# One router kernel, one change: first tiles' rows gathered singly, last routing steps moved forward

## The chip, the core and the metric

The kernel runs on one core of a Trainium2 chip. A core has five engines with an instruction stream each: TensorE (PE, matrix products), VectorE (DVE), ScalarE (ACT), GpSimd (POOL) and SyncE (SP, here used to start transfers). They meet only through semaphores. The metric is the device time of one execution in microseconds (us), lower is better; a kernel's time is the median of its runs.

## What is computed

A block with adaptive layer norm on 2048 tokens of width 512, all in float32: a small state layer (`tanh(h B^T) C^T + D h`), then a mixture of experts with 8 experts of width 352, of which each token takes two, and a shared part of two halves, each as wide as an expert.

```
mod = (silu(c) @ wmod).reshape(.., 6, 1, -1)          # sa, ca, ga, sb, cb, gb
h = layernorm(x) * (1 + ca) + sa
x = x + ga * (tanh(h @ B.T) @ C.T + D * h)
h = layernorm(x) * (1 + cb) + sb
scores = sigmoid(h @ gate_w.T);  idx = top_k(scores + router_bias, 2)
w = scores[idx] / sum(scores[idx])
y_e = (silu(h @ W1[e]) * (h @ W3[e])) @ W2[e]
x = x + gb * (sum over the two of w * y_e + shared(h))
```

## The kernel before

The 2048 tokens are 16 tiles of 128, worked in 8 pairs. Each float32 product is made of three matmuls of high and low parts (hi*hi, hi*lo, lo*hi), so each operand is split into a high part by ACT and a low part by DVE before TensorE can use it.

**Stage A** (to about 211 us) is a software pipeline over the pairs, `body(it, lo, hi)` on every engine, with iterations 0 to 10. In iteration `it` the pair `it-2` gets its state product and its second norm (`h2`), the pair `it-3` its transposes of h2 (`transposes`, L905), the split of the result (ACT `xah`, DVE `xal`), and the first shared half: `up`, `silu`, product `gbuf`, transposes of `g` (`turn_g`, L943), split `gth`/`gtl`, `down`. The pair `it-4` is routed: on DVE `route` in 12 small steps (0 to 6 before, 7 to 11 behind the matmuls of `ranks` on TensorE), which gives the rows to which POOL scatters the tokens of the pair in the DRAM tensor `xs` (`scatter`, four indirect DMAs a pair, L601). The rows of h2 to scatter are read back by SyncE into `hrow` (L406). In the last iteration POOL also starts the weights of the first expert: `raw` (2.2 MB) and the high parts `whi` in three pieces (`hi_part`).

**Stage B** is four steps, tiles 0 to 3 with the second shared half. Step 0 still has the last A tile's down product, and the last pair's ranks and `route`. In step 1 DVE builds `table_rows`, in step 2 `table_rest` (16 small instructions; its last one raises `s_tab`, on which POOL's `low`, the low parts of the first expert's weights, waits). In step 3 TensorE transposes the first tile of the scattered rows, loaded by SyncE when all scatters have landed (L448, L389).

**Stage S** runs all the expert tiles, some 6.7 us a step, and stores each result to the DRAM tensor `ys`.

**Stage C** (from about 485 us) is twelve steps (c,j), pairs c = 2 to 7, j = 0, 1, with the second shared half of tiles 4 to 15. POOL gathers the two expert results of each tile, `tbuf` and `xtf`, 128 rows each (`gather`, L684). The rows of the tiles 0 to 3 of stage B (`rowb`, in `raw`) are gathered too (`gather_first`, L691), two gathers a tile. One step (c,j) on DVE, in program order: low part of the next tile (`tlo`, L1349), `gbuf` (L1596), half of a `finish_first` (tile t: half 0 waits for both gathers of the tile, half 1 ends it; the halves run in steps (3,1), (4,0), (4,1), (5,0), ... (7,0)), `gtl` (L1610), `finish` of the tile before (four instructions, L1560 to L1567), and `offsets`, which writes the row numbers of the next tile (`idx`, L1528) that POOL's next `gather` waits for. TensorE in a step: transposes of the next tile, `up`, `down` of the tile before, `turn_g`. ACT enters a loop (`Fori`) at step (4,0).

Every engine works its stream in the written order. All of POOL's DMAs share one software queue, SyncE's another.

Of the kernel before, what the change touches and what calls it, by code (L numbers as in the profile page):

```python
# [35 lines left out]
NT = T // P  # L36
# [15 lines left out]
CB = 2  # L52
# [25 lines left out]
def build(nc, x, ccol, wmod, bt, ct, dvec, gwt, rb, w_all, consts, out):  # L78
# [4 lines left out]
    with ExitStack() as ctx:  # L83
# [404 lines left out]
        def _(pool):  # L488
# [60 lines left out]
            def body(it, lo, hi):  # L549
# [54 lines left out]

                if routes(lo, hi):
                    scatter(it - 4, 0)
                if lo == NP + 2:
                    hi_part(0, lambda: pool.wait_ge(q["A", "up"], NT))
                    hi_part(1, lambda: None)
                    scatter(it - 3, 1)  # L610
                    hi_part(2, lambda: pool.wait_ge(q["A", "dn"], NT))
# [76 lines left out]
            def gather_first(t):  # L688
                pool.wait_ge(s_bidx, 1)
                for k in range(2):  # L690
                    pool.indirect_dma_start(rowb[t][:, k, :], None, ys[:, :],  # L691
                                            bass.IndirectOffsetOnAxis(ap=idxb[:, 2 * t + k:2 * t + k + 1], axis=0)
                                            ).then_inc(s_brow[t], 16)
# [3 lines left out]
            for t in range(NB):  # L697
                gather_first(t)
                if t % 2:
                    for j in range(2):  # L700
                        gather(CB + 1 + t // 2, j)
            with pool.Fori(CB + 1 + NB // 2, NP) as c:
                for j in range(2):
                    gather(c, j)


        @block.scalar
        def _(act):
            def high(i, j, src):
                act.wait_ge(q["S", "xt"], i * 2 + (j + 1))  # L710
                act.activation(xbh[:, j, :], src[:, :], ACT.Copy).then_inc(q["S", "xhi"], 1)  # L711

            def hidden(p, j, lo):
                n = p * 2 + (j + 1)
                act.wait_ge(q["A", "up"], n)
                if lo > 3 or j:
                    act.wait_ge(q["A", "g"], p * 2 + j)
                act.activation(s1[:, :], bank[2][:, E:E + F], ACT.Silu).then_inc(q["A", "silu"], 1)
                act.activation(lg[:, bass.ds(p * 2 + j, 1), :].rearrange("p a e -> p (a e)"), bank[2][:, 0:E],
                               ACT.Copy).then_inc(s_lg, 1)  # L720
                if lo == NP + 2 and j == 1:
                    high(0, 0, bank[6])
                act.wait_ge(q["A", "gt"], n)
                if lo > 3 or j:
                    act.wait_ge(q["A", "dn"], p * 2 + j)
                act.activation(gth[:, :], bank[4 + j][:, 0:FP], ACT.Copy).then_inc(q["A", "ghi"], 1)
# [36 lines left out]
            def body(it, lo, hi):  # L763
                if live(1, lo, hi):
                    turned(it - 1, lo)
                if live(3, lo, hi):
                    p = it - 3
                    act.wait_ge(s_h2T, p + 1)
                    if lo > 3:
                        act.wait_ge(q["A", "up"], p * 2)  # L770
                    for j in range(2):
                        act.activation(xah[:, j, :], h2_bank(lo, j)[:, :], ACT.Copy).then_inc(q["A", "xhi"], 1)
                    if lo > NP:
                        scores(p - 1)
                    if lo == 3:
                        first_weights(2)
                    hidden(p, 0, lo)
# [10 lines left out]
                if live(3, lo, hi):  # L788
                    hidden(it - 3, 1, lo)
                    if lo not in (NP, NP + 1):  # L790
                        scores(it - 3)
# [77 lines left out]
        def _(pe):  # L869
# [128 lines left out]
            def body(it, lo, hi):  # L998
                if live(1, lo, hi):
                    turn_t(it - 1, lo)  # L1000
                if live(3, lo, hi):
# [37 lines left out]
                if live(3, lo, hi):  # L1039
                    pe.wait_ge(s_lg, (it - 3) * 2 + 1)  # L1040
                    up("A", it - 3, 1, 0)
                if lo == NP + 2:
                    turn(0, 0, bank[6])
# [9 lines left out]
                if routes(lo, hi):  # L1053
# [36 lines left out]
            def step(i, j, c, sec):  # L1090
# [23 lines left out]
                up("S", i, j, off, [NW + 1, NW + 2] if sec == "B" else need_up)  # L1114
                if early:
                    next_turn()
                if first:
                    ranks(NP - 1)
# [31 lines left out]
        def _(dve):  # L1150
# [200 lines left out]

            def body(it, lo, hi):
# [6 lines left out]
                if live(3, lo, hi):  # L1359
                    p = it - 3  # L1360
                    for j in range(2):
                        dve.wait_ge(q["A", "xhi"], p * 2 + (j + 1))
                        dve.tensor_tensor(xal[:, j, :], h2_bank(lo, j)[:, :], xah[:, j, :].bitcast(F32),  # L1363
                                          ALU.subtract).then_inc(q["A", "xlo"], 1)
# [80 lines left out]
                if live(3, lo, hi):  # L1445
                    product_a(it - 3, 1, lo)
                if lo == NP + 2:
                    lows(0, 0, bank[6])
                if live(3, lo, hi):
# [3 lines left out]
                between(*range(KM + 1, KR))  # L1453
# [117 lines left out]
            def step(i, j, c, sec):  # L1571
# [13 lines left out]
                if sec == "B" and i * 2 + j == 2:  # L1585
                    table_rest()
# [7 lines left out]
                else:  # L1594
                    dve.wait_ge(q["S", "gt"], i * 2 + j)
                dve.tensor_tensor(gbuf[:, 0:F], s1[:, :], bank[3][:, 0:F], ALU.mult).then_inc(q["S", "g"], 1)  # L1596
                m = (c - CB) * 2 + j - 3 if sec == "C" else -1
# [4 lines left out]
                if first:  # L1602
                    route(NP - 1, NP + 3, *range(KM + 1, KR))
# [94 lines left out]
```

## Time and profile before

| what | value |
|---|---|
| median of 3 runs | 583.18 us (582.14 to 585.02) |
| profiled execution: its own time | 589.56 us |
| profiled execution: span | 587.9 us |
| busy in the span | PE 547.9 us (93%), DVE 303.7, POOL 260.7, ACT 178.2 |
| mean granted TensorE clock | 0.981 |
| DMA moved | 107.18 MB, mean 182 GB/s |
| longest ACT wait | s L849, 10.1 us, at 499 us |
| longest POOL wait | tbuf L684, 45.3 us, for the last store of stage S |

The times are all of one profiled execution unless a median is named; a row of a timeline is start, duration, engine, line, operation, output and input, and in square brackets how long the engine was idle before it and what released it. The profiled execution took 6.4 us longer than the median. PE is busy in tenths of 9 in all but a few of the 40 slices of the page: the first four or so, and the 35th and 36th, 500 to 529 us.

### The profile page before, as it was taken

What the parts mean: (1) busy time and instruction counts of PE and PEld (TensorE: products, weight loads), DVE (VectorE), ACT (ScalarE), POOL (GpSimd) and SP (SyncE); (2) the same over time, 40 slices, a digit from 0 to 9 for tenths busy, and PEclk for the clock granted to TensorE, in tenths of its full rate; (3) what the DMA queues carried; (4) which work ended last, traced back from release to release, by engine and by line L of the source; (5) the groups of instructions that cost most, each with busy time, mean ns of one, the idle gap of its engine ahead of it and who ended that gap; (6) DMA issues with size and microseconds to landing.
All of it is one profiled execution on the core that took longest, in us unless ns stands there. A gap on an engine that the chain in (4) does not pass through costs nothing.

```text
span 587.9 us, 11157 instructions
## 1 busy us (share of the span) xinstructions
PE 547.9 (93%) x3176; PEld 494.7 (84%) x3177; DVE 303.7 (52%) x633; ACT 178.2 (30%) x343; POOL 260.7 (44%) x219
## 2 busy tenths in 40 slices
PE   5986799999999898999999999999999999679995
PEld 2655788998899897899999999999999999579994
DVE  3589876686687567433222232222222222457886
ACT  1242345345524432123222332222322223112220
POOL 1598876667665527442053420162633002451331
PEclk9998999999999999999999999999999999798999
DMA  8988244332232578556266762548484223672644
GB/s 307 394 297 317 72 186 173 127 115 81 89 144 105 200 260 272 206 195 225 89 191 236 254 227 91 168 144 321 143 321 141 73 71 106 180 215 78 190 144 142
DMA packets 38040, 107.18 MB, mean 182 GB/s; under 512 B 4224, under 2 KB 4224, under 8 KB 36992
## 3 DMA queue, kind: packets, MB, share of 16 engines
q1 hardware_dynamic: 28288, 54.44, 26.8%
q0 software_dynamic: 9728, 52.43, 25.9%
q8 instruction: 14, 0.23, 0.2%
q14 instruction: 10, 0.08, 0.1%
HBM read 76.19 MB, written 30.67 MB: 182 GB/s over the span
## 4 chain that ended last, share of the span: by engine, by line
PE 77%; POOL 8%; issue 5%; DVE 4%; DMA 2%; another core or an unknown queue 1%; ACT 1%; SPq 0%; DVEq 0%; ACTq 0%; POOLq 0%
PE bank L922 14%; PE bank L923 13%; PE bank L924 13%; PE bank L938 7%; PE bank L936 7%; PE bank L937 7%; PE bank L905 5%; PE bank L943 4%; PE bank L874 2%; PE bank L876 2%; PE bank L875 2%; PE bank L883 1%; POOL xs_rows L601 1%; DMA x_all<-wmod 1%
## 5 line engine op out<-in xcount | busy, mean ns | idle before, releaser
L922 PE MATMUL bank<-whi,thi 128*128 (+1 forms) x416 | 140.9, 339 | 0.0
L923 PE MATMUL bank<-wlo,thi 128*128 (+1 forms) x416 | 136.1, 327 | 0.0
L924 PE MATMUL bank<-whi,tlo 128*128 (+1 forms) x416 | 135.6, 326 | 0.0
L531 POOL TENSOR_TENSOR wlo<-raw,whi 128x1408 f32 (+3 forms) x24 | 79.6, 3331 | 85.9 <-DMA whi<-w_all 74.4
L1596 DVE TENSOR_TENSOR gbuf<-s,bank 128x352 f32<-128x352 f32 x52 | 27.1, 521 | 112.2 <-ACT s L849 107.5
L936 PE MATMUL bank<-whi,gth 128*128 (+1 forms) x204 | 80.7, 396 | 3.3 <-DVE wlo L1320 2.0
L938 PE MATMUL bank<-whi,gtl 128*128 (+1 forms) x204 | 80.5, 395 | 0.0
L922 PEld LDWEIGHTS bank<-whi,thi 128*128 128x128 f32 x416 | 80.0, 192 | 0.0
L923 PEld LDWEIGHTS bank<-wlo,thi 128*128 128x128 f32 x416 | 79.9, 192 | 0.0
L937 PE MATMUL bank<-wlo,gth 128*128 (+1 forms) x204 | 79.8, 391 | 0.0
L924 PEld LDWEIGHTS bank<-whi,tlo 128*128 128x128 f32 x416 | 79.6, 191 | 0.0
L849 ACT ACTIVATE s<-bank 128x352 f32<-128x352 f32 x52 | 24.2, 466 | 165.4 <-PE bank L924 148.0
L1610 DVE TENSOR_TENSOR gtl<-bank,gth 128x384 fp32r<-128x384 f32 x52 | 29.0, 558 | 84.5 <-ACT gth L857 83.0
L857 ACT ACTIVATE gth<-bank 128x384 fp32r<-128x384 f32 x52 | 25.6, 492 | 100.8 <-PE bank L943 91.2
L684 POOL DMA_INDIRECT tbuf<-ys_rows,idx x12 | 11.5, 958 | 90.3 <-DMA ys_rows<-tmpa 45.3
L936 PEld LDWEIGHTS bank<-whi,gth 128*128 128x128 f32 x204 | 38.3, 188 | 9.5 <-DVE wlo L1320 2.3
L938 PEld LDWEIGHTS bank<-whi,gtl 128*128 128x128 f32 x204 | 38.3, 188 | 8.9
L905 PE MATMUL bank<-cst,h 128*128 128x128 f32 x272 | 41.8, 283 | 4.2 <-DMA h<-xs_rows 2.8
L922 PE MATMUL bank<-whi,xah 128*128 128x360 f32 (+1 forms) x128 | 42.4, 331 | 2.8 <-DVE xal L1363 2.7
L1349 DVE TENSOR_TENSOR tlo<-bank,thi 128x512 fp32r<-128x512 f32 x52 | 35.8, 689 | 17.6 <-ACT thi L711 17.2
L943 PE MATMUL bank<-cst,gbuf 128*128 128x128 f32 x204 | 34.1, 276 | 10.6 <-DVE gbuf L1596 9.4
L943 PEld LDWEIGHTS bank<-cst,gbuf 128*128 128x128 f32 x204 | 26.3, 140 | 20.8 <-DVE gbuf L1596 10.7
(199 smaller groups left out, 982.5 us busy)
## 6 DMA issues: line engine op xcount, KB each, us to landing
raw<-w_all POOLq DMA_DIRECT2D x8, 2176.0 KB, 9.3
whi<-w_all POOLq DMA_DIRECT2D x16, 704.0 KB
h<-xs_rows SPq DMA_DIRECT2D x36, 256.0 KB
ys_rows<-tmpa SPq DMA_DIRECT2D x36, 256.0 KB, 2.0
x_all<-wmod SPq DMA_DIRECT2D x6, 1024.0 KB, 8.5
whi<-w_all POOLq DMA_DIRECT2D x8, 768.0 KB, 4.8
hs_rows<-h SPq DMA_DIRECT2D x8, 512.0 KB, 3.0
h<-hs_rows SPq DMA_DIRECT2D x16, 256.0 KB
```

The costliest lines, as they stand in the source:

```text
L531: pool.tensor_tensor(wlo[:, bass.ds(off + (SH + a), b - a)], raw[:, a:b], whi[:, bass.ds(off + (SH + a), b - a)].bitcast(F32), ALU.subtrac ...
L905: mm = pe.transpose(dst[:, k * P:(k + 1) * P], src[:, k * P:(k + 1) * P], ident)
L922: pe.matmul(dst, xh[:, j, a], wh, start=(m == 0), stop=False)
L923: pe.matmul(dst, xh[:, j, a], wl, start=False, stop=False)
L924: mm = pe.matmul(dst, xl[:, j, a], wh, start=False, stop=(m == KD - 1))
L936: pe.matmul(dst, gth[:, a], wh, start=(m == 0), stop=False)
L937: pe.matmul(dst, gth[:, a], wl, start=False, stop=False)
L938: mm = pe.matmul(dst, gtl[:, a], wh, start=False, stop=(m == KF - 1))
L943: mm = pe.transpose(dst[:, m * P:(m + 1) * P], gbuf[:, m * P:(m + 1) * P], ident)
L1349: dve.tensor_tensor(xbl[:, j, :], src[:, :], xbh[:, j, :].bitcast(F32), ALU.subtract).then_inc(q["S", "xlo"], 1)
L1596: dve.tensor_tensor(gbuf[:, 0:F], s1[:, :], bank[3][:, 0:F], ALU.mult).then_inc(q["S", "g"], 1)
L1610: dve.tensor_tensor(gtl[:, :], bank[4][:, 0:FP], gth[:, :].bitcast(F32), ALU.subtract).then_inc(q["S", "glo"], 1)
```

## The change

- POOL's code for stage C: `gather_first(t)`, which issued both gathers of one of the tiles 0 to 3, and ran for two tiles in a row (four DMAs) ahead of a pair's gathers, becomes `gather_first(t, k)`, one DMA, placed behind each of the eight gathers of (3,0) to (6,1). The loop over the last pairs is written out.
- Iteration 9 of stage A: the transposes of the last pair's h2, and their splits on ACT and DVE, come in iteration 9 behind the second `up` rather than at the start of iteration 10. ACT's `scores` of the last pair comes ahead of `gth`.
- Iteration 10: the matmuls of `ranks(6)` and DVE's steps 7 to 11 of that pair are ahead of the down product. POOL issues the first two high parts of the first expert's weights ahead of the scatter of pair 6 rather than behind it.
- Stage B: `ranks(7)` and `route(7, 7..11)` are ahead of the turn and of `gbuf` in step 0. `table_rest` comes in step 1, right behind `gbuf`, rather than in step 2.

```diff
 (POOL, iteration 10)
+                if lo == NP + 2:
+                    hi_part(0, lambda: pool.wait_ge(q["A", "up"], NT))
+                    hi_part(1, lambda: None)
                 if routes(lo, hi):
                     scatter(it - 4, 0)
                 if lo == NP + 2:
-                    hi_part(0, lambda: pool.wait_ge(q["A", "up"], NT))
-                    hi_part(1, lambda: None)
                     scatter(it - 3, 1)
...
 (POOL, stage C)
             for j in range(2):
                 gather(CB, j)
-            for t in range(NB):
-                gather_first(t)
-                if t % 2:
-                    for j in range(2):
-                        gather(CB + 1 + t // 2, j)
-            with pool.Fori(CB + 1 + NB // 2, NP) as c:
+            for c in range(CB + 1, NP):
                 for j in range(2):
                     gather(c, j)
+                    n = (c - CB - 1) * 2 + j
+                    if n < 2 * NB:
+                        gather_first(n // 2, n % 2)
...
 (ACT, hidden)
+                if lo == NP + 1 and j == 1:
+                    high_a(NP - 1, lo)
                 if lo == NP + 2 and j == 1:
                     high(0, 0, bank[6])
+                    scores(NP - 1)
                 act.wait_ge(q["A", "gt"], n)
...
 (PE, body)
+                if lo == NP + 1:
+                    pe.wait_ge(s_h2, NT)
+                    pe.wait_ge(q["A", "xlo"], NT - 2)
+                    pe.wait_ge(q["A", "glo"], NT - 3)
+                    for j in range(2):
+                        mm = transposes(h2_bank(lo, j), h2[:, j, :])
+                    mm.then_inc(s_h2T, 1)
                 if lo == NP + 2:
+                    ranks(it - 4)
                     turn(0, 0, bank[6])
...
 (PE, step)
+                if first:
+                    ranks(NP - 1)
                 if early:
                     next_turn()
                 if first:
-                    ranks(NP - 1)
                     last_tile(NP - 1, NP + 3)
...
 (DVE, body)
+                if lo == NP + 1:
+                    lows_a(NP - 1, lo)
                 if lo == NP + 2:
                     lows(0, 0, bank[6])
+                    between(*range(KM + 1, KR))
...
 (DVE, step)
-                if sec == "B" and i * 2 + j == 2:
-                    table_rest()
...
+                if first:
+                    route(NP - 1, NP + 3, *range(KM + 1, KR))
                 dve.tensor_tensor(gbuf[:, 0:F], s1[:, :], bank[3][:, 0:F], ALU.mult).then_inc(q["S", "g"], 1)
+                if sec == "B" and i * 2 + j == 1:
+                    table_rest()
...
                 if first:
-                    route(NP - 1, NP + 3, *range(KM + 1, KR))
                     finish_a(NP - 1, 1, NP + 3)
```

POOL's instructions of stage C, as the program before has them, from the gathers of (2,0) on (`tbuf` and `xtf` are a tile's two gathers, `raw` a gather of `gather_first`):

```order
L684 DMA tbuf<-ys_rows,idx 128x512
L684 DMA xtf<-ys_rows,idx 128x512
L684 DMA tbuf<-ys_rows,idx 128x512
L684 DMA xtf<-ys_rows,idx 128x512
L691 DMA raw<-ys_rows,idxb 128x512 x4
L684 DMA tbuf<-ys_rows,idx 128x512
L684 DMA xtf<-ys_rows,idx 128x512
```

and as the changed program has them:

```order
L685 DMA tbuf<-ys_rows,idx 128x512
L685 DMA xtf<-ys_rows,idx 128x512
L685 DMA tbuf<-ys_rows,idx 128x512
L685 DMA xtf<-ys_rows,idx 128x512
L685 DMA tbuf<-ys_rows,idx 128x512
L685 DMA xtf<-ys_rows,idx 128x512
L691 DMA raw<-ys_rows,idxb 128x512
L685 DMA tbuf<-ys_rows,idx 128x512
L685 DMA xtf<-ys_rows,idx 128x512
L691 DMA raw<-ys_rows,idxb 128x512
```

The four gathers that stood ahead of those of (3,0) are now one by one, each behind a tile's own two. The second gather of tile 0 stands behind the gathers of (3,1), where it stood ahead of (3,0).

DVE in steps 1 and 2 of stage B before (the first `tlo` is the low part of tile 2, `tqi` to the last `ti` is `table_rest`):

```order
L1596 TENSOR_TENSOR gbuf<-s,bank 128x352
L1349 TENSOR_TENSOR tlo<-bank,thi 128x512
L1610 TENSOR_TENSOR gtl<-bank,gth 128x384
L1533 TENSOR_TENSOR bank<-bank,mods 128x512
L1535 TENSOR_TENSOR x_all<-bank,x_all 128x512
L1349 TENSOR_TENSOR tlo<-bank,thi 128x512
L1296 TENSOR_SCALAR tqi<-tq 1x41
L1297 TENSOR_SCALAR ti<-tq 1x40
...
L1314 TENSOR_SCALAR ti<-tr 1x10
L1596 TENSOR_TENSOR gbuf<-s,bank 128x352
```

and in the changed program:

```order
L1616 TENSOR_TENSOR gbuf<-s,bank 128x352
L1310 TENSOR_SCALAR tqi<-tq 1x41
...
L1328 TENSOR_SCALAR ti<-tr 1x10
L1363 TENSOR_TENSOR tlo<-bank,thi 128x512
L1631 TENSOR_TENSOR gtl<-bank,gth 128x384
L1553 TENSOR_TENSOR bank<-bank,mods 128x512
L1555 TENSOR_TENSOR x_all<-bank,x_all 128x512
L1363 TENSOR_TENSOR tlo<-bank,thi 128x512
L1616 TENSOR_TENSOR gbuf<-s,bank 128x352
```

All of `table_rest` now stands between `gbuf` of step 1 and the low part of tile 2.

## Rows read from the trace of the kernel before

**Rows 1.** Timeline of PE, 195 to 245 us: start us, us, instruction, [idle before <-releaser]

```profile
198.01 0.40 PE L922 MATMUL bank<-whi,xah 128*128 128x360 f32 x1 [1.80 <-DVE xal L1363]
...
234.61 1.09 PE L905 MATMUL bank<-cst,h 128*128 128x128 f32 x4 [2.77 <-DMA h<-xs_rows]
...
240.28 0.39 PE L936 MATMUL bank<-whi,gth 128*128 128x512 f32 x1
...
242.69 0.60 PE L905 MATMUL bank<-cst,h 128*128 128x128 f32 x4
```

**Rows 2.** One-microsecond windows: busy us (instructions) by engine, PEclk, DMA share, GB/s

```profile
198.00:199.00 1.00, 0.99 (x6) 1.00 (x7) 0.57 (x2) 0.97 (x3) 0.92 (x1) 1.00 1.04 401
...
236.00:237.00 1.00, 1.00 (x5) 1.00 (x5) 0.50 (x1) 0.40 (x1) 1.00 (x2) 0.50 0.03 8
```

**Rows 3.** Timeline of DVE, 224 to 231 us

```profile
224.30 0.68 DVE L1349 TENSOR_TENSOR tlo<-bank,thi 128x512 fp32r<-128x512 f32 x1
...
228.11 0.17 DVE L1296 TENSOR_SCALAR tqi<-tq 1x41 int32<-1x41 f32 x1
...
230.22 0.50 DVE L1596 TENSOR_TENSOR gbuf<-s,bank 128x352 f32<-128x352 f32 x1
```

**Rows 4.** Timeline of POOL, 202 to 217 us

```profile
202.92 0.59 POOL L496 DMA_DIRECT2D raw<-w_all  x1
...
215.55 1.00 POOL L601 DMA_INDIRECT xs_rows<-mods,idx  x1 [12.03 <-DVE oh L1226]
```

**Rows 5.** Timeline of SyncE's DMA queue, 205 to 206 us

```profile
205.56 0.38 SPq L406 DMA_DIRECT2D mods<-hs_rows  x1
```

**Rows 6.** Chain that ended last, 225 to 235 us: start us, us, what

```profile
225.86 4.95 DMA xs_rows<-tmpa,idx
...
231.81 2.67 DMA h<-xs_rows
```

**Rows 7.** Timeline of ACT, 498 to 528 us

```profile
509.19 0.46 ACT L849 ACTIVATE s<-bank 128x352 f32<-128x352 f32 x1 [10.09 <-remote]
...
527.70 0.46 ACT L849 ACTIVATE s<-bank 128x352 f32<-128x352 f32 x1 [7.29 <-remote]
```

**Rows 8.** Timeline of PE from 497 us: the transposes of g

```profile
497.54 0.49 PE L943 MATMUL bank<-cst,gbuf 128*128 128x128 f32 x3
...
510.26 0.90 PE L943 MATMUL bank<-cst,gbuf 128*128 128x128 f32 x3 [5.87 <-DVE gbuf L1596]
...
528.77 0.90 PE L943 MATMUL bank<-cst,gbuf 128*128 128x128 f32 x3 [3.02 <-DVE gbuf L1596]
...
558.35 0.49 PE L943 MATMUL bank<-cst,gbuf 128*128 128x128 f32 x3
...
571.73 0.49 PE L943 MATMUL bank<-cst,gbuf 128*128 128x128 f32 x3
```

**Rows 9.** Timeline of DVE, 501 to 552 us

```profile
501.80 0.75 DVE L1560 SCALAR_TENSOR_TENSOR tmpa<-tbuf,wts,bank 128x512 f32<-128x512 f32 x1 [2.65 <-issue]
...
545.96 0.56 DVE L1610 TENSOR_TENSOR gtl<-bank,gth 128x384 fp32r<-128x384 f32 x1 [0.58 <-ACT gth L857]
546.43 0.74 DVE L1560 SCALAR_TENSOR_TENSOR tmpa<-tbuf,wts,bank 128x512 f32<-128x512 f32 x1
...
549.33 0.21 DVE L1528 CAST idx<-pos 128x1 uint32<-128x1 f32 x2
...
550.27 0.52 DVE L1596 TENSOR_TENSOR gbuf<-s,bank 128x352 f32<-128x352 f32 x1
...
551.22 0.75 DVE L1543 SCALAR_TENSOR_TENSOR raw<-raw,wts 128x512 f32<-128x512 f32 x1
```

**Rows 10.** Timeline of POOL, 550 to 553 us

```profile
550.30 1.01 POOL L684 DMA_INDIRECT tbuf<-ys_rows,idx  x1 [4.10 <-DVE idx L1528]
551.61 1.18 POOL L684 DMA_INDIRECT xtf<-ys_rows,idx  x1 [0.30 <-issue]
```

**Rows 11.** Half-microsecond window, columns as in group 2

```profile
555.00:555.50 0.50, 0.50 (x5) 0.50 (x5) 0.47 (x2) 0.00 (x0) 0.00 (x0) 1.00 0.00 0
```

## What I expect of the change

> **What bounds the kernel now.** I read the page's slices first, then the waits, then the timelines of the places where PE is not busy. PE is busy for 547.9 of 587.9 us, so a change can gain only where PE waits, and can lose wherever it makes PE wait. Three places matter.
>
> At 198.01 PE has waited 1.80 us for the low part of the last pair's h2 [rows 1]; the granted clock stayed at 1.00, 2.4 GHz [rows 2]. At 234.61 it has waited 2.77 us for the first tile of scattered rows, which SyncE loads when the last scatter has landed [rows 1, 6]. The clock fell there: 0.50 in 236 to 237 us, 1.2 GHz [rows 2]. From this turn to the next down product it took 240.28 - 234.61 = 5.67 us; at full clock it is a step of 6.69 less 242.69 - 240.28 = 2.41, so 4.28. The slow clock cost 1.4 us on top of the wait.
>
> In stage C, PE's transposes of g came 12.72 us apart at 510.26, and the two steps after that took 18.51 us, where two undisturbed ones take 571.73 - 558.35 = 13.38 [rows 8]. From 497.54 to 571.73 there are nine steps: 74.19 us, where 9 x 6.69 = 60.2 are due, so 14.0 us are lost. In both disturbed steps it is ACT's `silu` that came late, at 509.19 and 527.70, and what it waited for is no engine ("remote") [rows 7]. I take it for ACT's own code being fetched by DMA while POOL keeps the DMA engines busy: the first wait ends when the traffic of POOL's ten gathers in a row does, the second begins at ACT's entry into its loop and ends with the traffic of the next eight. The Trainium skill (Runtime: NRT & Kernel Launch, Instruction fetch mechanics) says that each engine streams its code over a DMA queue of its own and that a taken branch out of the loaded pages forces a fetch before work goes on; by that rule, too, fewer gathers ahead of the fetch shorten the wait, and the loop entry keeps one.
>
> **The change, front part (stages A and B).**
>
> 1. The last h2 transposes, one product earlier. TensorE does the same eight transposes, ACT's two splits fall in the time in which it waits for `gt`, DVE's two in its wait for the down product. So the wait of 1.80 us goes [rows 1]: -1.80 at 198 us. The clock had not fallen, so nothing is to be had from it.
>
> 2. `table_rest` in step 1. It takes 230.22 - 228.11 = 2.11 us [rows 3], and now stands ahead of the low part of tile 2, which `up` of step 2 waits for. Before, that low part started at 224.30, right behind `gbuf`, and ended at 224.98. Now it is 224.30 - 1.80 + 2.11 + 0.68 = 225.3. That gives back the 1.80: of step 1 some 0 to 0.2 us stay, I take 0.1. PE is then free for the first scattered tile at 234.61 - 2.77 - 0.1 = 231.7.
>
> 3. The scatters. POOL's queue has the 2.2 MB `raw` from 202.92, SyncE reads the rows of pair 6 from 205.56, and the scatter of pair 6 starts at 215.55 [rows 4, 5]. DVE's row numbers are put down as its releaser, but those of pair 6 had been there for two microseconds; I take the rows' landing for it, 10.0 us behind their issue, because both transfers share the engines. Routing earlier (ranks, steps 7 to 11) is then worth nothing for pair 6. And two `whi` pieces, 1.4 MB, are now queued in those ten microseconds instead of between the scatters. The rows' load also moves by some 0.8 us, since pair 5's routing stands behind the splits moved in 1. So pair 6 can start at 216.4 at the earliest and, if all of `whi` must pass first (3.6 us at the 401 GB/s of a busy window, [rows 2]), at 220; I take 217. The eight scatters take 225.86 + 0.96 - 215.55 = 11.3 us to issue [rows 4, 6], of which some 1.5 are the two `whi` issues between them: 226.8. Before, the last landed 4.0 us behind its issue (4.95 less 0.96, [rows 6]), behind 1.4 MB of `whi`. Those are gone, and pair 5's landed in 205.56 - 202.92 = 2.6 [rows 4, 5]: 229.4. SyncE's start and load cost 3.7 more, as before (231.81 + 2.67 against 230.8): 233.1, so the turn comes 1.5 us earlier than 234.61. The remaining gap, 1.4 us, is under the 1.80 that left the clock alone, so the 1.4 of the slow clock comes back as well. Front part: **-2.9**. Best case, everything in time at 231.7: -4.3. Worst, 220 + 9.8 + 4.0 + 3.7 = 237.5: +2.9.
>
> Stage S runs at PE's pace, 6.69 us a step, and passes that on unchanged.
>
> **The change, stage C.** The ten gathers in a row become four, and six from there on come in threes. In the frame of the trace before:
>
> 4. Step (3,0). `finish` of (2,0) still starts at 501.80, `idx` 2.90 later (546.43 to 549.33, [rows 9]), `gbuf` 0.94 after that: 505.6. ACT, with four gathers ahead instead of ten, should have its code by then. PE's transposes come at 506.2 rather than 510.26, and the clock should hold. `gtl` comes 1.9 us behind `gbuf` (turn_g, ACT's `gth`, hand-overs), `finish` 0.47 behind it [rows 9], so `idx` of (3,1) at 510.9.
>
> 5. A new wait, and it is the main thing. Half 0 of `finish_first` in step (3,1) waits for both gathers of tile 0. The second is now issued behind the two gathers of (3,1), and those wait for the `idx` that DVE has written at the end of the step before. So DVE waits, in the middle of its step, for three gathers that it has itself only just let go; behind this wait are queued `gtl` (PE's down), `finish`, `idx` and the next `gbuf`. The same holds for tiles 1, 2, 3 in (4,1), (5,1), (6,1). In us from `idx`: POOL starts 0.97 later (550.30 - 549.33); the two gathers need 551.61 + 1.18 - 550.30 = 2.49 [rows 10], the third 1.25: 4.71. Landing: the second gather of this pair was issued by 552.79 and no byte moves after 555.0 [rows 11], so 2.2: at 6.9. Bounds 1.7 (the same half-microsecond window) and 4.0 (the last scatter, [rows 6]). At present half 0 is done at 551.22 + 0.75 and starts some 0.43 behind `gbuf`'s start, 1.4 us behind `idx` [rows 9]; so DVE stands still for 5.5.
>
> 6. The period of two steps. From 6.9: half 0 ends 1.27 later (551.97 less 550.70, [rows 9]), `finish` starts 0.47 later, `idx` 2.90: 11.55. `gbuf` 0.94: 12.5. `gtl` 1.9 (half 1 fits in): 14.4. 0.47 and 2.90: 17.75. This is a closed loop of DVE and POOL, **17.75 us for two steps against 13.38** of PE. PE waits some 2.2 us for `gtl` and 2.2 for `gbuf` in each. Three such periods from 510.9 give `idx` of (6,1) at 564.15; `gbuf` of (7,0) at 576.65, transposes 0.55 later at 577.2 against 571.73: **+5.5** in which the removed 14.0 are already counted.
>
> 7. The clock in these gaps. 1.80 us left it, 2.77 did not; 2.2 twice, 2.1 us apart, lies between. I take it to fall. Most of that hides behind the loop, which doesn't contain `up`; the last `up`, behind (7,0), isn't hidden: +1.4, bounds 0 and 2.1 (18.51 - 13.38 - 3.02, what the clock cost after 510.26).
>
> The Trainium skill (DMA: Bandwidth & Descriptors, Anatomy of one DMA) gives some 2.0 us plus bytes over 436 GB/s for one DMA of GpSimd, 2.6 us for 262 KB; counted from the issue's start that is 1.65 behind its end, and the sum would be 2.2 us lower.
>
> **Sum.** -2.9 + 5.5 + 1.4 = +4.0 us: span 591.9, and that execution 593.6. The median of the runs is 6.4 below the profiled execution; if nothing of this is in the places above, the median goes from 583.18 to **587.2**. If part of ACT's two waits is longer only under the profiler, there is less to gain and as much to lose, so the error from this is upward.
>
> **Rivals.**
> - *Faster: the third gather lands almost at once.* With each gather issued in 0.95 and the third landed 1.0 behind its issue, each of the four waits is 1.5 us shorter: 4 x 1.5 = 6.0, so -2.0, and the clock holds: -3.4, **579.8**. For it: spaced gathers have the DMA engines nearly to themselves. Against it: the last pair's traffic ran for 2.2 us. It decides from a landing under 1.2 us.
> - *Even: same loop, cheap ends.* Landing 1.7, clock holds, front best: 5.5 - 2.0 - 4.3 = -0.8, **582.4**.
> - *ACT's late code has nothing to do with the gathers*, so the change doesn't do what it says: `gbuf` of (3,0) stays at 509.7, 4.1 later, and the loop follows: **591.3**. Against it: both waits end with the gathers.
> - *Landing 4.0*, with SyncE's loads and stores in the way: 4 x 1.8 = 7.2 more, **594.4**.
>
> **How the numbers follow.** Forecast 0.40, faster 0.17, even 0.25, ACT unchanged 0.10, slow landing 0.08. About 0.5% is what a measurement of this kernel tells from no change, 2.9 us; the forecast is at 0.7%, and I put 0.06 of it within. So slower 0.52, same 0.31, faster 0.17. The range goes from 579.5, just past the faster case, to 593.0, short of slow landing.
>
> **What would show it.** In the trace of the changed kernel: no idle PE near 196; a wait of 1.7 us at `up` of step 2; the first scattered tile's turn at about 233; ACT's `silu` of (3,0) within 505; DVE waits of some 5.5 us at L1561, four of them, each two steps apart; PE's transposes of g 17.7 us apart by twos. The prediction is wrong if these four waits are under 4 us, if a fetch of ACT's still ends later than the third gather, or if the scattered tile comes later than 234.6.

## The result, and the profile of the changed kernel

| | kernel before | changed kernel |
|---|---|---|
| median of 4 runs | 584.10 us (582.14 to 587.17) | 594.12 us (593.92 to 594.86) |
| profiled execution, own time | 589.56 us | 593.92 us |
| its span | 587.9 us | 592.3 us |

The ratio is **1.0169, with a 95% interval of [1.0121, 1.0217]**: slower, as forecast, but 594.12 us lies above the forecast of 587.2 and 1.1 us above the range. Span against span the change cost 592.3 - 587.9 = 4.4 us, where the sum said 4.0. That the two agree so closely is partly luck, since misses of the sum's terms cancel, but the loop that sets the end came as described. What failed is the step from the profiled execution of before to the medians: the median rose by 10.0 us, not by 4.0.

The page of the changed kernel: span, busy times, PE's busy tenths and the granted clock in 40 slices.

```profile
span 592.3 us, 11140 instructions
PE 548.8 (93%) x3176; PEld 492.5 (83%) x3177; DVE 302.9 (51%) x633; ACT 178.4 (30%) x343; POOL 259.3 (44%) x219
...
PE   5986799999999997999999999999999999887885
...
PEclk9998999999999999999999999999999999999799
```

PE's holes now lie in the last six slices; before they were in the 35th and 36th. In DVE's waits (engine, line, releaser: us in total, times, longest) there is an entry that the kernel before doesn't have:

```profile
DVE raw L1561 <- DMA raw<-ys_rows,idxb: 21.6, 4, 6.0
```

The same four in DVE's timeline (columns as in [rows 9]):

```profile
517.23 0.48 DVE L1561 TENSOR_SCALAR raw<-raw,wts 128x512 f32<-128x512 f32 x1 [5.97 <-DMA raw<-ys_rows,idxb]
...
534.67 0.49 DVE L1561 TENSOR_SCALAR raw<-raw,wts 128x512 f32<-128x512 f32 x1 [5.66 <-DMA raw<-ys_rows,idxb]
...
552.20 0.49 DVE L1561 TENSOR_SCALAR raw<-raw,wts 128x512 f32<-128x512 f32 x1 [5.74 <-DMA raw<-ys_rows,idxb]
...
570.12 0.49 DVE L1561 TENSOR_SCALAR raw<-raw,wts 128x512 f32<-128x512 f32 x1 [4.25 <-DMA raw<-ys_rows,idxb]
```

They end 17.44, 17.53 and 17.92 us apart: the period of two steps, forecast as 17.75. POOL's timeline shows the other half of the loop:

```profile
528.59 0.94 POOL L685 DMA_INDIRECT tbuf<-ys_rows,idx  x1 [2.17 <-DVE idx L1548]
529.84 0.95 POOL L685 DMA_INDIRECT xtf<-ys_rows,idx  x1 [0.30 <-issue]
531.10 0.95 POOL L691 DMA_INDIRECT raw<-ys_rows,idxb  x1 [0.30 <-issue]
```

DVE's `idx` lets three gathers go; the third, for which DVE then stands, is issued from 531.10 on. The chain that ended last says when such gathers landed (start us, us from issue to landing):

```profile
513.21 4.00 DMA raw<-ys_rows,idxb
531.10 3.55 DMA raw<-ys_rows,idxb
```

The second is 531.10 + 3.55 = 534.65, and DVE goes on at 534.67. PE pays twice in each period, once for `gtl` and once for `gbuf`. Its transposes of g, and the down product that waits for `gtl` (these are the rows that answer to [rows 8]):

```profile
497.57 0.49 PE L948 MATMUL bank<-cst,gbuf 128*128 128x128 f32 x3
...
505.25 0.55 PE L948 MATMUL bank<-cst,gbuf 128*128 128x128 f32 x3 [0.83 <-DVE gbuf L1616]
...
519.11 0.49 PE L941 MATMUL bank<-whi,gth 128*128 x1 [2.17 <-DVE gtl L1631]
...
523.07 0.55 PE L948 MATMUL bank<-cst,gbuf 128*128 128x128 f32 x3 [1.62 <-DVE gbuf L1616]
...
540.51 0.55 PE L948 MATMUL bank<-cst,gbuf 128*128 128x128 f32 x3 [1.61 <-DVE gbuf L1616]
...
558.04 0.90 PE L948 MATMUL bank<-cst,gbuf 128*128 128x128 f32 x3 [0.88 <-DVE gbuf L1616]
...
575.97 0.55 PE L948 MATMUL bank<-cst,gbuf 128*128 128x128 f32 x3 [1.61 <-DVE gbuf L1616]
```

From 497.57 to 575.97 there are nine steps, 78.40 us; in [rows 8] the same nine took 74.19. ACT's `silu` never waits for "remote" here; the row that answers to the first of [rows 7] stands at 502.38, not 509.19, and waits for PE:

```profile
502.38 0.47 ACT L854 ACTIVATE s<-bank 128x352 f32<-128x352 f32 x1 [3.25 <-PE bank L929]
```

In the front part, first POOL's scatter of pair 6 ([rows 4]), then PE's `up` of step 2 and the turn of the first scattered tile ([rows 1]):

```profile
217.75 1.13 POOL L601 DMA_INDIRECT xs_rows<-mods,idx  x1 [9.78 <-DMA mods<-hs_rows]
```

```profile
225.47 0.40 PE L927 MATMUL bank<-whi,thi 128*128 128x352 f32 x1 [1.76 <-issue]
...
234.42 0.94 PE L910 MATMUL bank<-cst,h 128*128 128x128 f32 x4 [2.47 <-DMA h<-xs_rows]
...
242.71 0.49 PE L910 MATMUL bank<-cst,h 128*128 128x128 f32 x3
```

The wait at 198 us is gone, the 1.76 us at 225.47 are new (due to `table_rest`), and the turn stands 0.19 us earlier than before. The turn after it is at 242.71, where it was at 242.69: the front part brought nothing.

### The profile page after: what moved, and what is told of

It is laid out like the page before. It is cut to its first block, busy times and chain, and to the rows that moved or that the text cites. A ratio compares the mean times of both kernels' runs of the same rounds, so it can differ in the third digit from the quotient of the medians.

```text
span 592.3 us, 11140 instructions
## 1 busy us (share of the span) xinstructions
PE 548.8 (93%) x3176; PEld 492.5 (83%) x3177; DVE 302.9 (51%) x633; ACT 178.4 (30%) x343; POOL 259.3 (44%) x219
## 4 chain that ended last, share of the span: by engine, by line
PE 68%; POOL 10%; DMA 8%; DVE 7%; issue 6%; ACT 1%; SPq 0%; DVEq 0%; POOLq 0%; ACTq 0%
PE bank L927 12%; PE bank L928 12%; PE bank L929 12%; PE bank L943 6%; PE bank L941 6%; PE bank L942 6%; PE bank L910 4%; PE bank L948 3%; DMA raw<-ys_rows,idxb 3%; DMA mods<-hs_rows 2%; PE bank L881 2%; PE bank L879 2%; PE bank L880 2%; POOL xs_rows L601 2%; PE bank L888 1%
## 5 line engine op out<-in xcount | busy, mean ns | idle before, releaser
L942 PEld LDWEIGHTS bank<-wlo,gth 128*128 128x128 f32 x204 | 38.5, 189 | 6.1
```

Of the source, the lines that this page charges most:

```text
L942: pe.matmul(dst, gth[:, a], wl, start=False, stop=False)
```

## Experiments

Theory 1 is that the loop of DVE and POOL is the whole cost and the front part is worth nothing. In its first form, held for `b_again`, `g_only`, `f_only` and `g_ahead`, it still counted most of the 14.0 us lost in [rows 8] as part of the kernel before, so it put the loop at 1.5% to 1.9% and expected a gain from the single gathers placed ahead; both were missed. From `b_again2` on it says that the 14.0 us belong to single executions, not to the kernel, and that the loop costs some 17.5 us against an execution without them. The rival keeps the prediction's reading: ACT's late code is part of the kernel before, brought about by its bursts of gathers. "Late code" stands here for ACT's two waits for "remote" in [rows 7]; that code is what ACT waited for is the prediction's reading. The experiments ran on three chips (that of the first comparison is not on record), each kernel beside runs of the kernel before, to which its ratio refers.

### The kernel before, unchanged, profiled again

> The kernel before, unchanged, profiled a second time. Its first profiled execution took 589.56 us where its runs have a median of 584.1; the changed kernel's profiled execution took 593.92, its median 594.12. Theory 1: the difference lies in the two waits of ACT for its own code in stage C, whose length differs from execution to execution. Then an execution near 583 shows PE's transposes of g from the end of stage S to (7,0) in about 68 us rather than 74.2, and the front up to the first scattered tile unchanged at 234.6. Theory 2: the difference lies in the front part (start, scatters): then the 74.2 stay and the first scattered tile's turn is some 6 us earlier.

576.31 us, span 574.7, against 589.56 and 587.9. Its ACT and PE (columns as in [rows 7] and [rows 8]):

```profile
501.04 0.47 ACT L849 ACTIVATE s<-bank 128x352 f32<-128x352 f32 x1 [3.25 <-PE bank L924]
```

```profile
496.23 0.49 PE L943 MATMUL bank<-cst,gbuf 128*128 128x128 f32 x3
504.81 0.55 PE L943 MATMUL bank<-cst,gbuf 128*128 128x128 f32 x3 [1.73 <-DVE gbuf L1596]
...
558.47 0.49 PE L943 MATMUL bank<-cst,gbuf 128*128 128x128 f32 x3
```

The ten gathers stand in a row, and no `silu` is late. Nine steps take 62.24 us, so 2.0 are lost and not 14.0. Of the 13.2 us between the two spans, 74.19 - 62.24 = 11.9 lie in these nine steps and 1.3 ahead of them (497.54 against 496.23). So the place is the one theory 1 named, but the execution is shorter by more than either theory had expected. The rival falls here: a burst of gathers alone doesn't make ACT's code late.

> The kernel before once more. Its first profiled execution had ACT's silu at 13.5 and 10.8 us instead of 6.7 us behind the one before it at two steps of stage C, and 14.0 us lost there; its second (b_again) had neither, 2.0 us lost, and was 13 us shorter. If the late code belongs to single executions, this one shows anything between: 2 to 14 us lost over the nine steps from (2,1) to (7,0), and its own time is 574 plus what is lost over 2.0. If something else makes the kernel's times differ, the lost time and the execution's own time do not move together.

On another chip 575.92 us, span 574.3; its nine steps take 558.07 - 496.51 = 61.56 us, so 1.4 are lost, just under the 2 to 14 expected.

> The kernel before, unchanged, a third look. Two looks in the experiments had no late ACT code and spans of 574.3 to 574.7 us. Theory 1 (the 14.0 us that the first profiled execution lost to ACT's late code belong to single executions, not to the kernel): this look too is either free of them, span 573 to 576 us, or, if the late code shows, its span is 10 to 14 us longer with ACT's first wait near 499 us. Rival (the late code is a steady part of the kernel that the two looks missed by chance): it shows, at 499 us and at the entry into the loop.

On a third chip 575.47 us, span 573.8: 557.64 - 495.13 = 62.51 us for the nine steps, 2.3 lost. All three executions agree within 0.9 us of span, and none has a `silu` that is released by "remote". So the late code wasn't seen again. That it is not a steady part of the kernel is shown, on three chips; why the first profiled execution had it is not.

### The gathers alone

The kernel before, with only this, and with `gather_first(t, k)` issuing one gather where `gather_first(t)` issued two:

```diff
-            for t in range(NB):
-                gather_first(t)
-                if t % 2:
-                    for j in range(2):
-                        gather(CB + 1 + t // 2, j)
-            with pool.Fori(CB + 1 + NB // 2, NP) as c:
+            for c in range(CB + 1, NP):
                 for j in range(2):
                     gather(c, j)
+                    n = (c - CB - 1) * 2 + j
+                    if n < 2 * NB:
+                        gather_first(n // 2, n % 2)
```

> The kernel before with the changed gathers of stage C alone; the front as before. Theory 1 (the loop of DVE and POOL costs the time, the front is worth nothing): ratio 1.015 to 1.019, as the whole change, and four DVE waits of 4 to 6 us in stage C, two steps 17.5 us apart. Rival (the front part costs some of the 10 us): 1.005 to 1.012.

596.06 us (594.05 to 598.72) beside 577.70: ratio 1.0335 [1.0275, 1.0396], far above the 1.015 to 1.019 expected, the whole of the loss and more than the first comparison showed for the whole change. Its span, 592.4, is 17.7 above that of `b_again` on the same chip. In DVE's waits:

```profile
DVE raw L1538 <- DMA raw<-ys_rows,idxb: 23.6, 4, 6.3
```

### Half of them late

Tiles 0 and 1 as in the kernel above, tiles 2 and 3 ahead of the tile's own two gathers. Against that kernel:

```diff
-                    gather(c, j)
                     n = (c - CB - 1) * 2 + j
+                    if NB <= n < 2 * NB:
+                        gather_first(n // 2, n % 2)
+                    gather(c, j)
-                    if n < 2 * NB:
+                    if n < NB:
                         gather_first(n // 2, n % 2)
```

> The changed gathers on the kernel before, but for the tiles 2 and 3 each single gather stands ahead of its tile's two, so that only the tiles 0 and 1 are waited for. By the loop of DVE and POOL two of the four periods of two steps stay at 17.5 us and two fall back to 13.4: 8.5 us over the kernel before, ratio 1.013 to 1.018 where the whole of it gave 1.0335. If the waits were not what costs (the written-out loop, more DMAs a step), it stays near 1.03.

585.41 us, ratio 1.0148 [1.0121, 1.0176]. In DVE's waits two of the three are long, of 6.35 and 5.83 us; the third is 0.21:

```profile
DVE raw L1540 <- DMA raw<-ys_rows,idxb: 12.4, 3, 6.4
```

Two waits cost 583.5 - 574.3 = 9.2 us of span, four cost 17.7: 4.4 to 4.6 us of the end for each wait of some 5.9. By the medians it is 585.41 - 576.83 = 8.6 for two and 596.06 - 577.70 = 18.4 for four, 4.3 to 4.6 each. Half the waits cost half the time. A cause that goes with the number of gathers or with the written-out `Fori` loop alone would give both kernels the same time, since these two differ in nothing but the order of four gathers.

### All of them ahead

Against the kernel of "The gathers alone":

```diff
                 for j in range(2):
-                    gather(c, j)
                     n = (c - CB - 1) * 2 + j
                     if n < 2 * NB:
                         gather_first(n // 2, n % 2)
+                    gather(c, j)
```

> The kernel before with the eight single gathers, each placed ahead of the two gathers of its tile instead of behind them, so that both rows of tile t are gathered one step before DVE asks for them. If the four waits are what costs, they vanish, and with them the long bursts: two steps are 13.4 us apart throughout, about 2 us of the 14.0 stay at (3,0): in the profile 576 to 578 us of span, against the median of before a ratio of 0.985 to 0.992 (theory 1). If single gathers cost by themselves (three DMAs in each step against the DVE's finish), the ratio stays at 1.00 or above.

575.66 us, ratio 0.9996 [0.9963, 1.0029], span 572.8. The waits are gone as expected; the expected gain (0.985 to 0.992) is not there. DVE has no wait for `raw` at all. POOL and DVE in the same stretch:

```profile
505.18 0.94 POOL L690 DMA_INDIRECT raw<-ys_rows,idxb  x1 [0.30 <-issue]
508.45 0.96 POOL L684 DMA_INDIRECT tbuf<-ys_rows,idx  x1 [2.33 <-DVE idx L1525]
```

```profile
508.82 0.48 DVE L1538 TENSOR_SCALAR raw<-raw,wts 128x512 f32<-128x512 f32 x1
```

The gather that `finish_first` needs at 508.82 is issued at 505.18, ahead of the wait for DVE's next `idx`, which ends at 508.45. The same eight single gathers, between the same others, cost nothing when they stand two places earlier in the queue. They also gain nothing over the bursts: the expected gain was most of the 14.0 us, and the undisturbed kernel loses only 1.4 to 2.3.

### The front part alone

The changed kernel with POOL's code for stage C as it was before.

> The changed kernel with the old gathers of stage C: the front part alone. Its share by the changed kernel's trace: the turn of the first scattered tile at 234.42 against 234.61, so nothing: ratio 0.998 to 1.002. My prediction's term was -2.9 us: 0.995. Rival (whi ahead of the scatters delays them in undisturbed runs): 1.003 or more.

576.71 us, ratio 0.9992 [0.9965, 1.0019]. The turn, in PE's timeline:

```profile
225.24 0.40 PE L930 MATMUL bank<-whi,thi 128*128 128x352 f32 x1 [1.76 <-issue]
234.26 0.63 PE L913 MATMUL bank<-cst,h 128*128 128x128 f32 x4 [2.53 <-DMA h<-xs_rows]
```

The kernel before has its turn at 233.82, 234.91 and 233.22 in its three other executions: the same place. The front part moves steps around and meets the same transfers.

### The front part without the two `whi` pieces moved

Against the kernel of the section before (so with the old gathers too):

```diff
-                if lo == NP + 2:
-                    hi_part(0, lambda: pool.wait_ge(q["A", "up"], NT))
-                    hi_part(1, lambda: None)
                 if routes(lo, hi):
                     scatter(it - 4, 0)
                 if lo == NP + 2:
+                    hi_part(0, lambda: pool.wait_ge(q["A", "up"], NT))
+                    hi_part(1, lambda: None)
```

> The front part of the change with the two whi pieces back between the scatters; old gathers. If whi ahead of the scatter of pair 6 is what delayed it (217.75 against 215.55), it starts at 215.5 to 216 again. The last scatter then again lands behind 1.4 MB of whi, so the first scattered tile's turn comes within 0.5 us of the kernel before's: ratio 0.998 to 1.002. A ratio under 0.996 would mean that moving whi alone spoiled the front part.

579.91 us, ratio 1.0049 [1.0024, 1.0074], where 0.998 to 1.002 was expected. The scatter of pair 6 starts at 216.11, 1.5 us earlier than with the `whi` pieces ahead of it (217.58 in `f_only`), but the last one lands later, as the chain shows (start us, us to landing):

```profile
220.89 5.21 DMA whi<-w_all
226.23 5.38 DMA xs_rows<-tmpa,idx
232.62 2.61 DMA h<-xs_rows
```

5.38 from the start of the issue against 3.61 in the changed kernel. The turn comes at 235.36 with a gap of 3.05, and the granted clock falls to 0.50. So of the front part, moving `whi` ahead seems worth something: the two ratios are 0.57% or some 3 us apart, and the rest of the front part takes about as much away. The two were measured on different chips, and how much of the 3 us is this fall of the clock is not shown.

### Everything forward, the weights behind the scatters

The changed kernel with the gathers ahead, `table_rest` back in step 2, and POOL's `raw` and first two `whi` behind both scatters:

```diff
-                    fetch_raw(0)
...
-                if lo == NP + 2:
-                    hi_part(0, lambda: pool.wait_ge(q["A", "up"], NT))
-                    hi_part(1, lambda: None)
                 if routes(lo, hi):
                     scatter(it - 4, 0)
                 if lo == NP + 2:
                     scatter(it - 3, 1)
+                    fetch_raw(0)
+                    hi_part(0, lambda: pool.wait_ge(q["A", "up"], NT))
+                    hi_part(1, lambda: None)
```

> Single gathers ahead of each tile's two, the h2 transposes and the routing moved forward as in the changed kernel, but table_rest back in step 2, and raw and whi of the first expert issued only behind both scatters. If the rows of pair 6 land late because raw is in flight (10 us for 0.5 MB), they land in under 5 us now, the scatters start at 210 to 211, the last lands by 224, and the first scattered tile's turn comes without a wait at 229.7 to 231: 3 to 4 us less than before, ratio 0.992 to 0.996. If the load of the first scattered tile is slowed by raw instead, the wait of 2 us at the turn stays and the ratio is 0.997 to 1.001.

575.95 us, ratio 0.9990 [0.9972, 1.0008]: no difference that can be told. The chain:

```profile
207.02 3.08 DMA h<-hs_rows
210.10 0.96 POOL xs_rows L600
...
219.47 2.73 DMA xs_rows<-tmpa,idx
223.20 8.86 DMA h<-xs_rows
```

The scatter starts at 210.10, where it was 217.75 in the changed kernel, 217.58 in `f_only` and 216.11 with only the `whi` pieces moved back. The rows to scatter are not what it waits for here. They come with SyncE's load issued at 205.56 before and at 205.59 here; the last number is us from issue to landing, first before, then here:

```profile
mods<-hs_rows SPq DMA_DIRECT2D x1, 512.0 KB, 9.2
```

```profile
mods<-hs_rows SPq DMA_DIRECT2D x1, 512.0 KB, 3.5
```

So without `raw` they are there at 209.1, and pair 6's row numbers at 209.30. The 210.10 is the landing of another load, `h<-hs_rows`, for which POOL's code still waits at the place where `raw` stood. In the kernel before the rows landed at 205.56 + 9.2 = 214.8, and the scatter started 0.8 us later; in the changed kernel it is 216.96 and 217.75. This shows what the prediction had only taken: the rows' landing, slowed by the 2.2 MB, was what held pair 6. But the load of the scattered rows now runs beside `raw` itself and takes 8.86 us instead of 2.68, so the turn is at 232.20, with a gap of 2.46. In both places that were tried for the weights, a small load that is waited for stood beside them.

### The changed kernel again, and with its gathers ahead

> The changed kernel, unchanged. Theory 1 (its loop of DVE and POOL sets stage C in every execution, and only the kernel before has executions with and without late code): 594 to 597 us, as in its first runs (594.12) and as the kernel with the gathers alone (596.06), four DVE waits of 5.5 to 6 us for raw, and a ratio of 1.028 to 1.036 against the kernel before on the same chip, rather than the 1.017 of the first runs. Rival (the first chip was slower by some 1.5% for both kernels alike): the changed kernel comes at 585 to 588 us here, with a ratio of 1.015 to 1.020.

595.05 us (593.29 to 597.21) beside 578.11 (575.05 to 580.93, 13 runs): ratio 1.0312 [1.0266, 1.0357]. The changed kernel takes nearly the same in both comparisons, 594.12 and 595.05. It is the kernel before that differs: 584.10 in the first comparison, 578.11 here. A first chip that makes both kernels slower alike is ruled out with that.

> The changed kernel with the single gather ahead of each tile's two rather than behind, so that it is let go a step before DVE needs it; all the rest of the change stays. Theory 1 (the place of the gather is the whole loss, the front part is worth nothing): no DVE wait for raw over 1 us, 573 to 578 us, ratio 0.996 to 1.002. Rival (the front part and the gathers cost something together, for instance by code or transfers that fall into each other): ratio over 1.004.

579.09 us, ratio 1.0030 [1.0008, 1.0051]. The loss goes from 3.1% to 0.3% by the order of eight instructions; there is no DVE wait for `raw`. The rest is between what the theories said (up to 1.002, and over 1.004), and is not settled by the one trace. There the clock fell twice, at the turn (235.08, gap 2.67) and in (3,0):

```profile
506.97 0.55 PE L948 MATMUL bank<-cst,gbuf 128*128 128x128 f32 x3 [1.86 <-DVE gbuf L1616]
...
515.31 0.49 PE L948 MATMUL bank<-cst,gbuf 128*128 128x128 f32 x3
```

That is 8.34 us for a step of 6.69. No version beat the kernel before by more than its measurement can tell.

## Why the prediction was right and wrong

The way back from the trace, span against span, with the profiled execution of before: front 0.0, nine steps of stage C 78.40 - 74.19 = +4.2, and the rest +0.2.

The terms of the sum were -2.9, +5.5 and +1.4 and measured 0.0, +4.2 and, within the last 0.2, some +0.1. Their misses of +2.9, -1.3 and -1.3 nearly cancel, and that is luck.

- **Steps 1 and 2 held.** The wait at 198 us went, `up` of step 2 waits 1.76 us instead (1.7 forecast), the low part of tile 2 starts at 224.69, 0.4 us later than before, and so ends within 0.1 of the 225.3 forecast. Together nothing.
- **Step 3 held in its mechanism, not in its size.** Pair 6 starts at 217.75 (217 forecast) and waits for the rows. The last issue ends at 226.99 + 0.96 = 227.95 (226.8), the landing takes 2.65 more (2.6), and SyncE and the load 3.8 (3.7): 234.42 instead of 233.1. That left a gap of 2.47 instead of 1.4, and the clock fell as before: 0.0 for a forecast -2.9. What was missed is small, 0.75 us of start and 0.4 of issue, but it carried the gap over the 1.80 on which the -1.4 of the clock hung. Even that condition was too simple: in `after_again`, the same kernel, a gap of 2.57 left the clock up. The "10.0 us" from issue to landing in this step were 9.2 of landing and 0.8 until the first scatter.
- **Step 4 held in its number, not in its reason.** The transposes came at 505.25 (506.2), and ACT was in time. But it was in time with all ten gathers too, in `b_again`, `b_again2` and `b_again3`, so no run shows that fewer gathers did it.
- **Steps 5 and 6, the main thing, held.** Four waits of 5.97, 5.66, 5.74 and 4.25 us where 5.5 was forecast; the third gather lands 3.55 - 0.95 = 2.6 us behind its issue's end, 3.05 the first time, within the bounds of 1.7 and 4.0 (2.2 taken). The periods are 17.44 to 17.92 for 17.75. PE waits 2.17 and 1.62 in the first period, 2.2 and 2.2 forecast. The transposes of (7,0) come at 575.97 for 577.2, mostly since the first `idx` of the loop came at 509.7 rather than 510.9 (POOL's gathers of (3,1) start at 510.70): +4.2 for +5.5.
- **Step 7 was too dear.** The clock held through the first two periods and fell once, in the third, where the loop hid most of it: DVE's wait there was 4.25 us instead of 5.7, and the period 0.4 longer than the one before. The last `up` was at full clock: 582.39 - 575.97 = 6.42 us to the last transposes, 6.31 in `b_again`. So 0.1 for +1.4.
- **What failed is in the base.** This is the step that put the forecast out of its range. The prediction took the 14.0 us of [rows 8] for a property of the kernel ("in which the removed 14.0 are already counted") and then carried the 6.4 us between profiled execution and median over to the new kernel ("The median of the runs is 6.4 below the profiled execution"). The changed kernel has no such difference: its profiled execution took 593.92 and its median is 594.12. The 10.0 us by which the median rose are near the 4.0 of the sum and these 6.4 together. It named the direction of that error, "the error from this is upward", and kept its size out of both the sum and the range. By the three other executions the nine steps of before lose 1.4 to 2.3 us, not 14.0. The loop, priced against 62.24 rather than 74.19, costs 78.40 - 62.24 = 16.2 us, and the spans differ by 592.3 - 574.7 = 17.6. The changed kernel's four runs lie within 0.9 us. Its loop is there in each execution, so its median was to be forecast from its own profiled time, 593.6 by the prediction's sum of 591.9 and the 1.7 around it. The hint was in the table: the profiled execution was longer than the slowest of the three timed runs by 4.5 us, and its list of waits had one entry that none of the later ones has, ACT's `silu` released by "remote":

```profile
ACT s L849 <- remote: 17.4, 2, 10.1
```

- **The rival that came nearest did so by chance.** "Landing 4.0" gave 594.4, next to the measured 594.12, but its condition failed: the landings came 2.6 to 3.05 us behind the issue's end.
- **The rule of the Trainium skill** (Runtime: NRT & Kernel Launch, Instruction fetch mechanics) says that a branch out of the loaded code makes an engine wait for a fetch. The first trace has two waits that could be this, 10.09 and 7.29 us; `b_again` with the same gathers and the same entry into the loop has none. That a burst of gathers makes such a wait longer was the prediction's own inference, and no run here shows it. The Trainium skill (DMA: Bandwidth & Descriptors, Anatomy of one DMA) gives an estimate of 2.6 us for 262 KB. Counted from the issue's start that would be 1.65 behind its end, and the trace says 2.6 to 3.05; so the rows (2.2) were the nearer source.

**What stays open.** The four runs of before in the first comparison, 582.14 to 587.17 us, are 4.0 to 9.1 us above the 578.11 of a later one, and none of them has a trace; only the profiled execution, 589.56, has. Of the 55 runs of before in the three later comparisons only two are above 582 us. So whatever made the first ones long was there in all of them, and "single executions" is not shown: something that goes with that chip or that set of runs fits as well. That they hold one of ACT's two waits would fit too, but it is argued. Whether the waits are code at all is open. The first trace has packets of the kind "instruction": one begins between 498.5 and 499.0 and lasts 1.5 us, the next begins between 521.5 and 522.0 and lasts 1.0, and none of them ends near 509.19 or 527.70, where ACT goes on. The waits were in none of the later traces.

## What to carry to other kernels

Where an engine waits for a transfer that it has itself let go through another engine's queue, count the loop from issue to landing: a gather two places too far back in the queue cost 4.3 to 4.6 us of the end each time, and two places forward it cost nothing. Before a wait is counted as a gain, ask whether the median holds it: a profiled execution that is longer than every timed run, as 589.56 is here, may contain something that those don't, and waits released by no engine (here "remote") are candidates. A second profile of the same kernel answers it. When a change makes a new closed loop that sets the end, forecast its time from the loop up, not as the old median plus a difference.

## What was not expected of the hardware

- **The clock doesn't follow the length of one gap.** Gaps of PE after which it stayed at 2.4 GHz: 2.53 us (234.26, `f_only`), 2.57 (234.55, `after_again`), 2.04 (504.03, `b_again3`). Gaps after which it fell to 1.2 GHz: 2.47 (234.42, changed kernel) and 1.86 (506.97, `a_ahead`). The two executions of the changed kernel show it at the same place. In one-microsecond windows (columns as in [rows 2]), first the one that fell, then `after_again`:

```profile
236.00:237.00 1.00, 1.00 (x5) 1.00 (x5) 0.69 (x1) 0.05 (x1) 1.00 (x1) 0.50 0.09 23
```

```profile
236.00:237.00 1.00, 1.00 (x8) 1.00 (x8) 0.67 (x1) 0.00 (x0) 1.00 (x1) 1.00 0.46 51
```

A term of 1.4 us that hangs on a gap near 2 us is a toss, and belongs in the range, not in the sum.

- **A small load beside a large one.** SyncE's rows for pair 6, 0.5 MB, landed 3.5 us after their issue without POOL's 2.2 MB beside them (`best1`), 8.4 to 9.2 with it (the kernel before, four executions), and 11.2 with 1.4 MB of `whi` beside it as well (changed kernel, `f_only`). SyncE's load of scattered rows took 8.86 us beside `raw` (`best1`) against 2.68 without. The loads stand in different queues, SyncE's and POOL's, and still slow each other.
- **A wait for what the trace calls "remote", taken for late code, was in one execution only.** It took 10.09 and 7.29 us there, and three others of the same kernel, on three chips, have nothing of the kind.
